# First tile loads and warm-up matmuls of a gated cross-attention block: two token tiles on two DMA queues, six warm-ups in place of eight

## The reference

```python
# layer 0
mem    = ctx @ W_mem.T                                  # 512 x 256
attn   = softmax(x @ mem.T / sqrt(256)); c = attn @ mem
gate   = sigmoid(concat(x, c) @ W_gate.T + b_gate)
x      = rmsnorm(x + gate * c, norm_w)
# layer 1, 16 heads of 64
q      = layernorm(x) @ Wq / 8;  k, v = split(ctx @ Wkv)
x      = x + tanh(attn_gate) * (softmax(where(mask, q k^T, min)) v) @ Wo
x      = x + tanh(ff_gate) * gelu(layernorm(x) @ W1) @ W2    # 256 -> 1024 -> 256
```

## Time and the profile before

| | us |
|---|---|
| three runs | 214.29, 214.09, 511.52; median 214.29 |
| the profiled execution, its own time | 214.26 |
| its span in the trace | 212.4 |
| outside the span | 1.9 |
| PE busy in the span | 206.2 |

### The profile page before, as it was taken

How to read it: one execution, slowest core, us unless ns; L and a number is a source line. 1 busy time by engine, 2 the same in 40 slices (tenths; PEclk the granted TensorE clock), 3 DMA queues, 4 the chain that set the end, 5 groups by cost and what they waited for, 6 DMA issues and landing times.

```text
span 212.4 us, 4471 instructions
## 1 busy us (share of the span) xinstructions
PE 206.2 (97%) x1491; PEld 168.6 (79%) x1491; DVE 149.9 (71%) x527; ACT 128.1 (60%) x411; POOL 71.2 (34%) x70
## 2 busy tenths in 40 slices
PE   7999999999999999999999999999989999999993
PEld 3577746998679888888988798888767899988993
DVE  1679888689988858796879679999948764234310
ACT  3368073689964683884694396997598740158300
POOL 2010043373647031526331524968031906000000
PEclk9999999999999999999999999999999999999999
DMA  6994500014000000000000000000600000100011
GB/s 201 332 361 148 197 0 2 3 14 185 3 0 2 3 2 0 5 2 0 3 2 0 3 2 3 0 0 5 197 2 3 0 0 29 51 25 0 11 45 57
DMA packets 8657, 10.06 MB, mean 47 GB/s; under 512 B 1074, under 2 KB 7732, under 8 KB 8372
## 3 DMA queue, kind: packets, MB, share of 16 engines
q1 hardware_dynamic: 7956, 9.32, 13.0%
q10 hardware_dynamic: 672, 0.39, 0.7%
HBM read 8.66 MB, written 1.05 MB: 46 GB/s over the span
## 4 chain that ended last, share of the span: by engine, by line
PE 83%; ACT 5%; DMA 3%; issue 3%; DVE 2%; SPq 1%; DVEq 0%; ACTq 0%
PE bank L435 47%; PE bank L1226 7%; PE bank L1198 7%; PE bank L1327 6%; ACT expd L667 4%; PE bank L1236 3%; DMA ctx_sb<-in_ctx_dram 3%; PE bank L1276 3%; PE bank L1290 3%; PE bank L1181 2%; SPq L473 1%; PE bank L1266 1%; PE bank L1106 1%; DVE oT_pair L991 1%; PE bank L1129 1%
## 5 line engine op out<-in xcount | busy, mean ns | idle before, releaser
L542 POOL TENSOR_TENSOR probs<-expd,row_rcp 128x512 f32<-128x512 f32 x39 | 41.8, 1092 | 64.0 <-DVE row_rcp L901 64.0
L667 ACT ACTIVATE expd<-expd,neg_max 128x128 f32<-128x128 f32 x128 | 49.6, 393 | 1.9 <-DVE neg_max L891 1.8
L891 DVE CUSTOM_DVE_ANT_0 expd<-bank,mask_bias 128x128 f32<-128x128 f32 x128 | 28.6, 285 | 4.3 <-PE bank L1198 2.6
L435 PE MATMUL bank<-wo_pair,oT_pair 128*128 128x256 f32 x192 | 26.8, 290 | 0.2 <-DVE x_sb L1017 0.2
L435 PE MATMUL bank<-xhT_pair,wq_pair 128*128 128x256 f32 x192 | 26.1, 287 | 0.0
L435 PEld LDWEIGHTS bank<-wo_pair,oT_pair 128*128 128x128 f32 x192 | 24.1, 190 | 2.4 <-issue 2.1
L435 PEld LDWEIGHTS bank<-xhT_pair,wq_pair 128*128 128x128 f32 x192 | 23.8, 191 | 1.4 <-DVE xhT_pair L961 0.6
L667 ACT ACTIVATION_READ_ACCUMULATOR expd<-expd,neg_max 128x1 f32 x128 | 24.5, 192 | 0.0
L435 PE MATMUL bank<-wq_pair,gelu_pair 128*128 128x256 f32 x192 | 23.6, 283 | 0.1
L435 PEld LDWEIGHTS bank<-wq_pair,gelu_pair 128*128 128x128 f32 x192 | 23.3, 192 | 0.4 <-DVE x_sb L1059 0.3
L1226 PE MATMUL bank<-ident,probs 128*128 128x128 f32 x160 | 21.4, 276 | 0.0
(11 more groups left out here) (147 smaller groups left out, 349.3 us busy)
## 6 DMA issues: line engine op xcount, KB each, us to landing
stage<-in_L_xattn_W_dram SPq DMA_DIRECT2D x2, 1024.0 KB, 5.0
x_sb<-in_x_dram SPq DMA_DIRECT2D x4, 256.0 KB, 7.5
wkv_sb<-in_L_xattn_Wkv_dram SPq DMA_DIRECT2D x2, 512.0 KB, 5.3
stage<-in_L_xattn_Wq_dram SPq DMA_DIRECT2D x1, 1024.0 KB, 9.1
stage<-in_L_xattn_Wo_dram SPq DMA_DIRECT2D x1, 1024.0 KB, 5.3
out_dram<-x_sb SPq DMA_DIRECT2D x8, 128.0 KB, 1.9
ctx_sb<-in_ctx_dram SPq DMA_DIRECT2D x4, 192.0 KB, 6.1
probs<-in_L_xattn_W_gate_dram SPq DMA_DIRECT2D x1, 512.0 KB, 7.7
```

The source lines that it names most:

```text
L435: last = nc.tensor.matmul(bank_ap, lhs(a), rhs(c), start=start and n == 0, stop=stop and n == 2)
L542: nc.gpsimd.tensor_tensor(probs[:, r, :].rearrange("p (h k) -> p h k", h=hb), expd[:, r, :].rearrange("p (h k) -> p h k", h=hb), row_rcp[: ...
L667: last = nc.scalar.activation(here, here, ACT.Exp, bias=neg_max[:, r, h:h + 1], scale=-1.0, accum_out=row_sum[:, r, h:h + 1])
L891: last = nc.vector.tensor_tensor_reduce(expd[:, r, h * w:(h + 1) * w], SC[n % 2][:, h * w:(h + 1) * w], mask_bias[:, first:first + w], -1. ...
```

## The change

- x of batch 0 comes in two loads of 128 KB: token tile 0 first on SP's queue, on `x_in[0]`; token tile 1 first on ACT's queue, ahead of W_mem and the context of batch 0, on a new semaphore `x0_rest_in`.
- The four transposes are ordered by token tile: wait for tile 0, its two transposes (k=0, k=1), wait for tile 1, its two. Each bank is signalled after its second tile.
- The warm-up is six matmuls. Their moving operand is the first 128 columns of `warm`, read four times by a stride of zero, so each still has 512 columns. The memset clears only these 128 bf16 columns.

```diff
-WARM_UP = 8
+WARM_UP = 6
...
+        x0_rest_in = sem("x0_rest_in")
...
-            load_x(0)
+            load(x_sb[:, 0, :], x[0, 0:P, :], x_in[0])
             load(mask_tiles[:, :], mask.rearrange("b (t n) -> (b t) n", n=P), w_in["tiles"])
...
         def _(sc):
 
+            sc.dma_start(x_sb[:, 1, :], x[0, P:N, :]).then_inc(x0_rest_in, 16)
             sc.dma_start(wmem_sb[:, :, :], w_mem.rearrange("(p k) e -> p k e", k=K)).then_inc(w_in["wmem"], 16)
...
-            nc.vector.memset(warm, 0.0).then_inc(warm_ready, 1)
+            nc.vector.memset(warm[:, 0:P], 0.0).then_inc(warm_ready, 1)
...
                     if st == ("xT", 0):
-                        te.wait_ge(x_in[0], 16)
-                        for k in range(K):
-                            free(path, st, k)
-                            for t in range(T):
+                        for t in range(T):
+                            te.wait_ge((x_in[0], x0_rest_in)[t], 16)
+                            for k in range(K):
+                                if t == 0:
+                                    free(path, st, k)
                                 last = nc.tensor.transpose(path.bank(st, k)[:, t * P:(t + 1) * P],
                                                            x_sb[:, t, k:D:K], ident[:, :])
-                            last.then_inc(pe["xT"], 1)
+                                if t == T - 1:
+                                    last.then_inc(pe["xT"], 1)
...
             for _ in range(WARM_UP):
-                nc.tensor.matmul(CONTEXT[:, :], warm[:, 0:P], warm[:, :], start=True, stop=True)
+                nc.tensor.matmul(CONTEXT[:, :].rearrange("p (a n) -> p a n", n=P), warm[:, 0:P],
+                                 warm[:, 0:P].rearrange("p (a n) -> p a n", a=1).to_broadcast([P, BANK // P, P]),
+                                 start=True, stop=True)
```

## The result

The changed kernel took 218.97 us (median of six runs, 218.94 to 219.78), the kernel before 214.24 beside it: a ratio of 1.0233, with a 95% interval of 1.0216 to 1.0249. I had forecast 214.2, in a range up to 215.8. The profiled execution took 219.78 us, 5.52 more than the one of before, with a span of 218.0.

A forecast was written before the change was run, and what follows sets the result against it. The start was taken as bound by the load of the rest of the context, landing at 11.08. TensorE arrives 0.1 us sooner and waits 0.45 instead of 0.35: gain 0, with a few hundredths for later order 214.2; range 213.7 to 215.8.

The forecast's parts named there:

- What bounds the start: First 11 us: the chain lies on the load of the rest of the context, landing at 11.08; TensorE has 0.35 us slack.
- Memset and warm-ups: TensorE's start: memset 0.17 us, warm-ups from 1.10, six at the old rate, PE free at 3.63 instead of 4.58.
- x and W_mem: First loads: tile 0 lands at about 3.7, tile 1 at 3.94, W_mem at 4.3 to 4.7; DVE's copy starts at 4.75.
- Context of batch 0: Load on ScalarE's queue: issued at about 1.72 instead of 1.22, landing taken as 5.5, between ends 5.02 and 6.4.
- The rule that I weighed: DMA queues: engines alternate between queues packet by packet, so the context's 512 B pieces against Wkv's 4 KB would land near 6.4.
- load stream gets shorter: Rival, loads of the start: with x over both queues the whole stream moves 0.4 us up, 213.85 us; chance 0.12.
- context lands late: Rival, load of batch 0's context: landing at 6.4, its transposes 1.1 us later, +0.45 us, 214.7; chance 0.15.
- clock comes up later: Rival, TensorE between 4.6 and 5.5 us: later clock rise leaves work at half speed, +1.15 us, 215.4; chance 0.23.
- within 2%: Whole kernel: time stays within 2% (4.3 us) of the kernel before; chance 0.97.
- the far end of the clock case: TensorE before 10.8 us: clock rises only at 10.8, doubling 5.28 us of work, at most 219; slower by 2% got 0.02.

The follow-up runs named there:

- value_later: The changed kernel with the hot context rows and the value half of Wkv exchanged on SyncE's queue, hot rows first; 219.69 us, ratio 1.0246.
- mask_on_act: The kernel before with only the 2 KB mask tiles load moved to ScalarE's queue, between W_mem and the context of batch 0; 218.10 us, ratio 1.0172.
- warm_only: The kernel before with six warm-ups on the narrow operand and the short memset, loads and transposes unchanged; 214.70 us, ratio 1.0013.
- both_on_sp: The changed kernel with tile 1 of x moved to SyncE's queue, behind tile 0; 216.12 us, ratio 1.0091.
- value_waits: The changed kernel with the value half of Wkv on SyncE's queue issued only after tile 0 of x has landed; 215.64 us, ratio 1.0072.
- two_on_sp_no_shift: The changed kernel with both tiles of x on SyncE's queue and the mask tiles third on ScalarE's queue; 216.80 us, ratio 1.0124.

## Why the prediction was wrong, point by point

- *What bounds the start.* The reading was right for the kernel before: the chain lay on a load, and TensorE had 0.35 us of slack. It was used wrongly. I took the landing at 11.08 as fixed and everything ahead of it as covered. Ahead of it stood three more loads that each landed within 0.3 us of their use: x (4.24, used at 4.31), the context of batch 0 (5.02, 5.22) and the hot rows (7.0, 7.24). A delay of any of them by more than the slack goes into the time.
- *Memset and warm-ups.* 0.11 us instead of 0.17, and six warm-ups at the old rate: start at 1.00, x transposes ready to start at 3.53. The operand with stride zero costs nothing that shows (2.53 us from 1.00 to 3.53). The bounds were worded the wrong way round: PE free at 2.4 is a doubled rate, at 6.2 a halved one.
- *x and W_mem.* Tile 0 landed at 0.74 + 2.6 = 3.3 (taken 3.7, bound 3.4), tile 1 at 0.74 + 2.8 = 3.5 (3.94), W_mem at 1.18 + 2.7 = 3.9 (4.3 to 4.7), DVE's copy started at 4.59 (4.75). All sooner than forecast, tile 0 even below its bound. These loads came across quicker, and the later ones slower.
- *Context of batch 0: the step that failed.* "I take 5.5", between the ends 5.02 and 6.4; it landed at 10.12, so the upper end of this term was 3.7 us too low. It was worked out as if only the 512 KB of one load could come in between, at the full 357 to 400 GB/s, and as if the context would start as soon as its queue had moved what stood ahead. Neither held. Its queue was clear at 3.4 us, and moved no packet until after 4.6. It moved its last between 9.0 and 9.5, and by 9.0 q1 had moved 1.39 MB, as much as tile 0, the mask tiles, the hot rows and both halves of Wkv together. In between it was slow: 299 packets from 5 to 7 (lines below), where before it had moved 660 - 129 = 531 in the 1.0 us from 3.4 to 4.4. And the two queues together moved 179 GB/s from 3 to 6 us. What the earlier trace rows showed was the context with its data ahead of Wkv's on the other queue. It was no bound for the context with Wkv ahead, and I used it as one. Why the data of the context came so late to start stays open.
- *The rule that I weighed.* The Trainium skill (DMA: Bandwidth & Descriptors, section "Queues, rings and completion order") has each DMA engine take turns between its queues. It pointed the right way, that the context would be late, and I gave it a seventh of the chance. The packets of value_later from 5 to 6 us agree with it, 105 on q10 and 98 on q1. It does not account for the stretch from 3.4 to 4.6 us of after, in which q10 moved none while q1 moved 43. The other sentence (section "Issuing engines are not separate DMA queues"), that a second queue saves only issue time, is not all that happened here: moving a 2 KB load to the other queue cost 3.9 us in mask_on_act.
- *The rival "load stream gets shorter".* It went the other way: by 10.5 us both queues had moved 2.42 MB, against 2.78 in before.
- *The rival "context lands late".* Right in mechanism and in place, mis-sized in the term: transposes 1.1 us late forecast, 4.84 measured, and +0.45 us of time forecast, 4.73 measured.
- *The rival "clock comes up later".* There were two effects of the clock, not one. Much as forecast, in warm_only: `y` at half speed, 1.29 us later at the transposes of the rest of the context (I had 1.6 before the slack), for 0.8 us at most at the end by the interval, where I had 1.15. That it came with six warm-ups in this execution and not in both_on_sp makes it a matter of the execution too. As not forecast, in after: the clock fell in the 5.6 us of idle time, at a price of 1.2 to 2.0 us. When it first came up the windows do not tell, since they read 1.00 from the start in both kernels.
- *Chances.* 0.97 for "within 2%" rested on the far end of the clock case being the only road to 4.3 us. A second wait that reaches into the first wait's cost wasn't among the cases: the late load caused the slow clock, and I had priced each alone.

The queues of after between 5 and 7 us (packets, MB, share of 16 engines), to the step that failed:

```profile
q1 hardware_dynamic: 256, 0.39, 57.4%
q10 hardware_dynamic: 299, 0.15, 27.6%
```

Both queues moved data there, and the two together less than q1 alone did in the same two microseconds of before (0.73 MB).

## What to carry to other kernels

Where several loads land just before their use, a change in the order of issues is not priced by its bytes: look for every load that stands near the moved one on the other queue, in time of issue or with its data, and give the moved load a bound taken from a run in which it has a neighbour, or else a wide one. Check each following load in its turn, since the cure of the first wait showed the second. A long wait ahead of matmuls (5.6 us in after) costs its own length and the slower clock behind it. A short one need not: behind the 2.59 us of value_waits the scores took 1.88 us, against 1.98 in the earlier trace rows.

## What the runs showed of the hardware that I had not expected

- Moving 2 KB of mask tiles between two queues made a 256 KB load take 7.1 us instead of 3.8, with the other loads unchanged in size. The 2 KB load itself took 4.0 us there, and 5.7 us as third on ScalarE's queue in two_on_sp_no_shift, against 2.5 on SyncE's queue in after.
- A queue can stand still with loads issued and nothing ahead of them: in after, q10 moved no packet from 3.4 to 4.6 us, with the context issued at 1.66.
- Total bandwidth was 179 GB/s from 3 to 6 us in after, against 367 in before, in a stretch in which both queues had loads issued. A late context does not need that: in mask_on_act it was 305 GB/s, and the context landed at 8.8 all the same. The cause was not found.
- With 512 B pieces on one queue and 4 KB pieces on the other, the queues moved about as many packets each (105 and 98 from 5 to 6 us in value_later), so the one with small pieces moved 0.05 MB of the 0.23 of both.
- The granted clock fell to 0.50 while TensorE stood idle, and the rows show it: at 5 to 7 us it still read 1.00, at 8 to 10 us 0.50.
